# Self-attention scores from two float32r halves on half the rows of the array, two heads at a time, with the mask matmul ahead

## What is computed

```python
def _mha(xn, kv_src, Wq, bq, Wk, bk, Wv, bv, causal):
    q = jnp.einsum('btc,hcd->bhtd', xn, Wq) + bq[None, :, None, :]
    k = jnp.einsum('bsc,hcd->bhsd', kv_src, Wk) + bk[None, :, None, :]
    v = jnp.einsum('bsc,hcd->bhsd', kv_src, Wv) + bv[None, :, None, :]
    scores = jnp.einsum('bhtd,bhsd->bhts', q, k) / DH ** (-0.5)
    if causal:
        scores = jnp.where(mask[None, None], scores, -jnp.inf)
    attn = jax.nn.softmax(scores, axis=-1)
    return ...  # attn @ v, heads side by side
xn1 = _ln(x, g1, be1)
x = x + (_mha(xn1, xn1, ..., causal=True) @ W1 + b1)
x = x + (_mha(_ln(x, g2, be2), encoder_out, ..., causal=False) @ W2 + b2)
x = x + jax.nn.relu(_ln(x, g3, be3) @ Wf1 + bf1) @ Wf2 + bf2
```

## Time and profile before

| | us |
|---|---|
| median of 3 runs | 627.89 (627.78 to 629.59) |
| span of the profiled execution | 631.5 |
| PE busy | 504.7 (80%) |
| DVE busy | 368.2 (58%) |
| ACT busy | 307.5 (49%) |
| POOL busy | 187.8 (30%) |

### The profile page before, as it was taken

How to read it: one execution, slowest core, us unless ns; L and a number is a source line. 1 busy time by engine, 2 the same in 40 slices (tenths; PEclk the granted TensorE clock), 3 DMA queues, 4 the chain that set the end, 5 groups by cost and what they waited for, 6 DMA issues and landing times.

```text
span 631.5 us, 8807 instructions
## 1 busy us (share of the span) xinstructions
PE 504.7 (80%) x3296; PEld 296.2 (47%) x3296; DVE 368.2 (58%) x695; ACT 307.5 (49%) x590; POOL 187.8 (30%) x276
## 2 busy tenths in 40 slices
PE   1775775999997999799988835669576757989887
PEld 0664452344443444344333333434222446988877
DVE  4887697678886788678532147645221763454430
ACT  3544020667765776477666502247443535253460
POOL 3788821131221132122132523305131350121200
PEclk9988697799999999899999969767555968999998
DMA  8138936007367335727260266978333212101001
GB/s 288 47 109 158 201 116 118 0 21 116 52 120 105 67 66 107 115 56 38 83 186 1 68 168 92 173 108 140 107 99 115 81 47 72 34 0 34 18 17 34
DMA packets 41930, 56.51 MB, mean 89 GB/s; under 512 B 12832, under 2 KB 27424, under 8 KB 41888
## 3 DMA queue, kind: packets, MB, share of 16 engines
q1 hardware_dynamic: 39584, 47.56, 38.1%
q10 hardware_dynamic: 2304, 8.39, 3.8%
HBM read 35.12 MB, written 20.42 MB: 88 GB/s over the span
## 4 chain that ended last, share of the span: by engine, by line
PE 44%; DMA 23%; DVE 15%; ACT 6%; SPq 5%; issue 3%; POOL 2%; ACTq 0%; DVEq 0%
PE ps L864 10%; PE ps L973 9%; PE ps L948 8%; PE ps L911 7%; DMA arena_h<-heads 6%; DMA stacks<-shift_t 6%; PE ps L1060 5%; DMA recips<-recip_rows 4%; DVE max_a L1141 4%; ACT arena_p L732 4%; DMA heads<-out_t 4%; DVE xn L1094 3%; SPq L409 2%; PE ps L933 2%; SPq L428 2%
## 5 line engine op out<-in xcount | busy, mean ns | idle before, releaser
L732 ACT ACTIVATE arena_p<-ps 128x512 f32<-128x512 f32 (+4 forms) x416 | 190.9, 541 | 129.5 <-PE ps L948 127.3
L1141 DVE TENSOR_REDUCE max_a<-ps 128x1 f32<-128x512 f32 (+4 forms) x280 | 159.6, 620 | 46.6 <-PE ps L911 34.0
L948 PE MATMUL ps<-stacks 99*128 99x512 bf16 (+2 forms) x448 | 149.9, 369 | 27.6 <-DMA stacks<-shift_t 22.5
L911 PE MATMUL ps<-stacks 96*128 96x77 bf16 (+4 forms) x640 | 146.2, 306 | 32.1 <-DVE max_a L1141 19.1
L911 PEld LDWEIGHTS ps<-stacks 96*128 96x128 bf16 x640 | 58.9, 111 | 97.5 <-DVE max_a L1141 45.5
L973 PE MATMUL ps<-arena_p,v_group 128*32 128x512 f32 (+4 forms) x896 | 94.1, 540 | 0.7 <-POOL arena_p L617 0.5
L617 POOL TENSOR_SCALAR_AFFINE_SELECT arena_p<-arena_p 128x512 f32<-128x512 f32 x64 | 41.0, 653 | 169.9 <-ACT arena_p L732 169.9
L948 PEld LDWEIGHTS ps<-stacks 99*128 99x128 bf16 (+1 forms) x448 | 45.6, 107 | 93.1 <-ACT arena_p L732 37.8
L1141 DVE TENSOR_REDUCE max_b<-ps 128x1 f32<-128x384 f32 (+3 forms) x88 | 52.5, 636 | 21.3 <-PE ps L915 21.3
L864 PE MATMUL ps<-wf2r,hid_r 128*128 128x256 f32 x384 | 49.9, 294 | 9.6 <-DVE hid_r L1254 9.6
L864 PEld LDWEIGHTS ps<-wf2r,hid_r 128*128 128x128 f32 x384 | 49.1, 202 | 10.7 <-DVE hid_r L1254 10.7
(11 more groups left out here) (68 smaller groups left out, 528.1 us busy)
## 6 DMA issues: line engine op xcount, KB each, us to landing
heads<-out_t ACTq DMA_DIRECT2D x16, 512.0 KB, 4.3
stacks<-q_parts SPq DMA_DIRECT2D x48, 128.0 KB, 5.2
stacks<-k_parts SPq DMA_DIRECT2D x48, 128.0 KB, 7.6
stacks<-qc_parts SPq DMA_DIRECT2D x48, 128.0 KB, 5.1
arena_h<-heads SPq DMA_DIRECT2D x8, 512.0 KB
recips<-recip_rows SPq DMA_DIRECT2D x8, 512.0 KB
q_parts<-parts SPq DMA_DIRECT2D x8, 384.0 KB, 2.5
k_parts<-parts SPq DMA_DIRECT2D x8, 384.0 KB, 2.6
```

The lines of the kernel that those rows point to most:

```text
L732: nc.scalar.activation(probs[0:a.kp, a.probs_slot(g, ui), h, k * BANK:k * BANK + width], ps[0:a.kp, unit % S_BANKS, 0:width], ACT.Exp, sca ...
L911: ins = nc.tensor.matmul(m_bank(use)[:, o:o + w], q_stack[0:ROWS, g % a.nb, h, t * P:(t + 1) * P], k_rows(ROWS, g, h, s0, s0 + w), start=T ...
L948: ins = nc.tensor.matmul(ps[0:keys, unit % S_BANKS, lo - k * BANK:hi - k * BANK], k_rows(ROWS_S, g, h, i * P, i * P + keys), q_stack[:, g ...
L1141: nc.vector.tensor_reduce(dst, m_bank(use)[:, 0:nh * w].rearrange("p (h w) -> p h w", h=nh), AX.X, ALU.max).then_inc(s.max_read, 1)
```

## The change

q and k are kept as two float32r halves (high and the rest) instead of three bf16 parts: three products of halves, 48 rows, plus 2 rows for the negated maximum. Even heads lie on partitions 0 to 49, odd heads on 64 to 113, so that two heads can stand in the two 64-row halves of the array. Units and chunks come in pairs, an even head and an odd head. The chunks become 40 in 20 pairs. `chunk_pair` writes the mask first, for both banks, and then the scores onto it; it waits once for both banks. `split` needs one ACT and one DVE instruction and none on POOL; `split_shift` three instead of five. Each load is 16 partitions by 2 x 1024 float32 instead of 4 x 1024 bf16, as many loads as before. The ones in k are set by two POOL memsets of 32 partitions that now stand early, and one memset for the context stands in group 6. The shift goes in four transfers instead of three.

```diff
-        self.units = [(ui, h, k) for ui, (_, width) in enumerate(self.steps)
-                      for h in range(GH) for k in range(-(-width // BANK))]
+            self.units = [(ui, 2 * hp + e, k) for ui, (_, width) in enumerate(self.steps)
+                          for hp in range(PAIRS) for k in range(-(-width // BANK)) for e in range(2)]
...
+                    nh = min(BANK // w, PAIRS)
+                    self.chunks += [(t, list(range(2 * hp + e, GH, 2))[:nh], s, w)
+                                    for hp in range(0, PAIRS, nh) for e in range(2)]
...
-                while stream and stream[0][0] <= g + unit_at[u] + lead:
+                while (not self.causal or u % 2 == 0) and stream and stream[0][0] <= g + unit_at[u] + lead:
                     use(stream.pop(0)[1])
+                    if self.causal and stream and self.uses[-1][0] == "chunk" and self.uses[-1][2] % 2 == 0:
+                        use(stream.pop(0)[1])
...
+            def load_halves(src, dst, which, g, arrived):
+                for e in range(2):
+                    for blk in range(len(QH)):
+                        r = TILE * e + blk * D
+                        sp.dma_start(dst[r:r + D].bitcast(F32), src[which[blk], g].rearrange("(p e d) t -> e d p t", e=2, d=D)[e])\
+                            .then_inc(arrived, 16)
...
             low_half(0)
+            pool.wait_ge(xn_low_a, KC)
+            for e in range(2):
+                made(pool.memset(k_self[TILE * e + 32:TILE * (e + 1), :, :, :].bitcast(F32), 1.0))
+                pool.wait_ge(consts, 9 + e)
             ln_root(2)
...
-            third_parts(*range(0, 4))
...
+                    nc.scalar.activation(parts_r[:, u % 3, HI, :], src, ACT.Identity, bias=col[:, c:c + 1])\
+                        .then_inc(split_a, 1)
+                    return
...
                     elif c == 3 or c == 0 and n:
-                        pe.wait_ge(split_a, 2 * (u - 3 if c else u - 1) + 2)
+                        pe.wait_ge(split_v, v_cnt(u - 3 if c else u - 1))
...
+                def chunk_pair(use, g, c):
...
+                    at_least(pe, s.max_read, use + 1 - M_BANKS + 1)
+                    if diagonal:
+                        for e in range(2):
+                            nh = len(a.chunks[c + e][1])
+                            to = m_bank(use + e)[:, 0:nh * w].rearrange("p (h w) -> p h w", h=nh)[:, :, w - P:w]
+                            nc.tensor.matmul(to, identb[:, :], maskb[:, :].rearrange("p (o q) -> p o q", o=1)
+                                             .to_broadcast([P, nh, P]), start=True, stop=False, skip_group_check=True)
+                    for e in range(2):
+                        hs = a.chunks[c + e][1]
+                        r = slice(TILE * e, TILE * e + ROWS_H)
+                        for j, h in enumerate(hs):
+                            ins = nc.tensor.matmul(m_bank(use + e)[:, j * w:(j + 1) * w],
+                                                   q_self[r, par, h // 2, t * P:(t + 1) * P],
+                                                   k_self[r, par, h // 2, s0:s0 + w], start=not diagonal, stop=True,
+                                                   skip_group_check=True)
+                        ins.then_inc(s.max_full, 1)
...
+                            if a.causal:
+                                r = slice(TILE * (h % 2), TILE * (h % 2) + ROWS_HS)
+                                lhs_t = k_self[r, g % a.nb, h // 2, i * P:i * P + keys]
+                                rhs = q_self[r, g % a.nb, h // 2, q0 + lo - off:q0 + hi - off]
...
+                    nc.vector.scalar_tensor_tensor(out=p[:, LO, :], in0=ps[:, unit_bank(u), 0:width],
+                                                   scalar=col[:, c:c + 1], in1=p[:, HI, :].bitcast(F32),
+                                                   op0=ALU.add, op1=ALU.subtract).then_inc(split_v, 1)
```

More of the change, by code:

```diff
@@ L46 @@
 ROWS_S = ROWS + PARTS
+HALVES = 2
+QH = [HI, HI, LO]
+KH = [HI, LO, HI]
+ROWS_H = D * len(QH)
+ROWS_HS = ROWS_H + HALVES
+TILE = 64
+PAIRS = GH // 2
 SCALE = float(D) ** 0.5
@@ L75, in __init__ @@
         self.kp = min(P, keys)
+        self.shift_ops, self.shift_dmas = (3, 4) if causal else (5, 3)
         self.steps = []
@@ L317, in build @@
         parts_out = [sem(f"parts_out{s}") for s in range(4)]
+        halves_out = [sem(f"halves_out{s}") for s in range(3)]
+        k_ones = sem("k_ones")
         wf1_halves, wf2_halves = sem("wf1_halves"), sem("wf2_halves")
@@ L632, in attention @@
                         ln_root((NCH if a.causal else 2 * NCH) + what[0])
+                    if op == "score" and a.causal and what[0] == NG - 2 and a.step_end(*what) == 1:
+                        pool.wait_ge(S1.scores, len(a.units) * (NG - 2))
+                        pool.wait_ge(S1.v_set, NG)
+                        pool.wait_ge(S1.masked, a.masks(NG - 2, 0))
+                        pool.memset(stacks[ROWS:ROWS_S, 5, :, :], 1.0).then_inc(k_ones, 1)
+                        pool.wait_ge(k_ones, 1)
                     if op == "score" and a.causal and a.step_end(*what) is not None:
@@ L985, in attention @@
                         kind, *of = a.uses[use]
+                        if a.causal and kind == "chunk":
+                            if of[1] % 2 == 0:
+                                chunk_pair(use, *of)
+                            continue
                         at_least(pe, s.max_read, use - M_BANKS + 1)
```

186 lines of the change are left out of this document (127 added, 59 removed).

## The result

The kernel after takes **757.46 us** (median of 4 runs, 755.51 to 760.5), the kernel before 628.74 beside it: **ratio 1.205, 95% interval 1.198 to 1.212**. The forecast was 658, with a range up to 685: the direction was right, the size was not. The profiled execution has a span of 753.6 us against 631.5, so 122.1 us have to be found. All ratios here are of undisturbed executions; only the profiled execution of a_ms, further on, is a slower, disturbed one (754.29 us against 741.95 to 750.27).

What follows compares the result with a forecast made beforehand. PE was taken to pace plain groups; with pairs waiting for two banks, they rise from 28.03 to 33.4 us. Attention +25.4 and work ahead of it +5 make about +30, so 627.9 becomes 658; range 616 to 685.

Steps and rivals of the forecast that it cites:

- rival (4): Attention: half-row matmuls leave PE at 1.2 GHz after the first wait, over 40 us per group, 720 and more; chance 0.07.
- The halves overlap: Units and chunks in attention: both array halves work at once, about 8 us less PE streaming per group; full overlap assumed.
- The bank wait: Chunk pairs in attention: each waits for two of three M banks, a plain pair's loop taking 1.30 us against DVE's 1.20.
- The weight load that nothing hides: First float32r matmul of a pair behind a bf16 matmul: 0.52 us instead of 0.39, so 0.13 more.
- Rival (1): Chunk pairs: weight load and tiling change hidden, 30.0 us per group with the drain, 27.8 without; weights hidden, chance 0.16.
- The change of tiling: Full-row masks ahead of half-row chunks in diagonal pairs: two changes of 0.09 us each per pair.
- DVE starves at products: Plain group: DVE idles after each product, which costs what exceeds PE's free 0.60 us, 5.0 us for six products.
- Rival (2): Attention: banks don't bind and DVE sets the pace, groups about 25.8 us, 617 in all; chance 0.15.
- Rival (3): Pairs in attention: halves do not overlap, the second 0.22 us later, +2.6 us per group, about 674; chance 0.07.
- Transfers of groups 2 and 4 hide under a longer group: Groups 2 and 4, stretched by transfers to 32.06 and 32.20 us: group 2 becomes 33.4 (+1.3), group 4 +1.2.
- Projections and all ahead of the first unit: Before the first unit: early memsets delay DVE, chunk pairs without units add +5 at worst; +5 us, ends 0 and +9.
- Group 7, +1: Last attention group, which has no chunks: 1 us longer.

Runs made afterwards that it cites:

- a_ms: The kernel after with its two POOL memsets of the key rows moved behind the first and second bias: 746.73 us, ratio 1.193 against the kernel before.
- m_clock: No attention, x copied to the output; six PE matmul loops paced by DVE reductions, behind dense matmuls or a pause: 1.34 to 1.55 us a turn.
- b_pairs: The kernel before, bf16 and 96 rows, with only self-attention chunks issued two at a time behind one wait for both banks: 656.78 us, ratio 1.039.
- the bare loop: No attention, x copied to the output; PE runs matmul patterns back to back without waits: twenty half-row pairs 4.71 us, twenty full-row matmuls 4.77.
- a_fill1: The kernel after with one pair of useless half-row matmuls behind each pair of units between a group's first and last product: 717.01 us, ratio 1.141.

## Why the prediction was wrong, step by step

- **The step that failed is the clock.** The sum priced every row at 2.4 GHz, and rival (4), "half-row matmuls leave it at 1.2 GHz", stood beside it with a chance of 0.07. Its price was right: "over 40 us per group: 720 and more", measured 44.4 and 757. Its reason was too narrow: not only half-row matmuls do it (m_clock's two full-row ones a turn lost the clock too), and here the level isn't low throughout but alternates. The evidence was in the earlier trace rows, with PE busy for all 12.00 us at 0.51; I read from it that busy time doesn't bring the clock, and didn't ask what does. The change lowers the array's work per us twice: each matmul fills 48 rows in a half, and pairs halve the time, while DVE's 22.5 us a group keep the length. Of the +98.1 us in groups 0 to 6, my terms make 24 (b_pairs 19). The other 74 I put down to the clock: 35 us of the loss come back with one pair of filler, in spite of the filler's own time and of a clock that is still at 0.88; for the rest it is argued, since no run had the change at the full clock throughout. An estimate speaks for it: groups 1 to 5 of the change lie near a line in their clock (47.4 us at 0.60, 44.4 to 44.6 at 0.69, 40.5 at 0.79), and drawn on to 1.00 it gives some 33 us, beside the 33.4 predicted.
- **The halves overlap:** right. 0.23 us a pair in the bare loop, 0.50 for both behind a wait.
- **The bank wait:** right in kind and size. Plain loop 1.28 (1.30 predicted). No group of the change itself has the full clock throughout; b_pairs, with the same wait but 96 rows and no masks ahead, has 32.7 us a plain group, and a_fill1 35.8 with its filler in, on both sides of the 33.4 predicted.
- **The weight load that nothing hides:** right, 0.50 for the first float32r pair where streaming is 0.39. Rival (1), all hidden, falls.
- **The change of tiling:** right in size, 0.11 for 0.09 in the bare loop, but counted once too often. At the full clock the chunks start 0.22 us behind the masks (391.43 to 391.65), of which two masks of 128 columns are 0.11 by my price. Where PE then waits for DVE, the change back falls into that wait, and the diagonal loops of 384 and 512 columns take 1.31 and 1.49 for the 1.40 and 1.59 predicted. Where more unit work stands in the loop (four matmuls, together 1.09 us), PE is the late one, and it does take 1.59 (380.79 to 382.38).
- **DVE starves at products:** right, 0.74 and 1.22 us idle at the full clock, and DVE is busy 24.0 for 22.5. Rival (2), DVE's pace, falls; its decisive loop of under 1.0 us never appears.
- **Rival (3), no overlap:** falls with the bare loop.
- **Transfers of groups 2 and 4 hide under a longer group:** right, 44.4 and 44.6 us beside the 44.4 of group 1.
- **Projections and all ahead of the first unit, +5 (0 to +9):** 17.5. The memsets were priced right, 5.2 us each for 5, and so was what they do: the third deviation 9.2 us late for some 8, the first pair of chunks 4.3 late for 3 to 4. That they hold DVE's own instructions was not foreseen and hardly changes this. The term that failed is the stretch of chunks without units, +13 for "+5 at worst": it was priced at the full clock and ran at 0.71, and one split, of those that were to give 1.5 back, waited 9.90.
- **Group 7, +1:** +6.9. Its units are pairs of half-rows as well; its clock is 0.81 and before it was 1.00.
- **After attention, nothing:** right, 279.3 us for 279.7.
- **The sign of being wrong was named:** "a granted clock under 0.9 for whole groups" is what every group from 0 to 7 shows (0.60 to 0.81).

## What to carry to other kernels

Packing two small matmuls into two halves of the array halves the time in which it works. If another engine sets the pace, the time isn't saved, and the granted clock can fall; then everything else on PE takes longer, the products here 2.36 us for 1.28. So before such a change, ask of each stage what will fill the array at the pace of the engine that waits last, rows as well as columns, and compare with a stage of the same profile whose clock is low. To learn whether a loss is the clock's, add useless matmuls where PE waits: a kernel that gets faster with more work has answered.

## What was unexpected of the hardware

- The granted clock fell when the matmuls used 66 rows instead of 96 (0.90 against 0.97), with the same time for each at the same clock, and further at 48 rows (0.61), with PE busy for 350.40 of 351.25 us. How rows and time are weighed against each other stays open: the kernel before with 48 rows came out lower (0.61) than the change (0.69), though it streams for longer.
- A dense stream in one half stayed at 0.50 for 55.56 us; dense pairs, 96 or 128 rows behind the same pause came up. But a loop of four 96-row matmuls a turn that kept 1.00 behind dense work stayed at 0.50 behind a pause: which level a loop has depends on the one it starts from.
- Useless matmuls made a kernel 40 us faster (757.46 to 717.01).
- A memset of 32 partitions on POOL held DVE's SBUF-to-SBUF instructions for its whole length: 5.38 us each for two that take 0.72 together without it.
